# The attribute products of a graph kernel on 64 rows each instead of 128

## What is computed

```python
xn = layernorm(x)
# graph layer: 100,000 edges
m   = concat([xn[src], edge_attr_3], axis=1)          # 256 + 3 columns
tmp = relu(m @ W1.T + b1)
h_N = segment_sum(tmp, dst, num_segments=3125)
gnn = normalise(relu(concat([xn, h_N], axis=1) @ W2.T))
# four layers of linear attention and a 1024-wide feed-forward part on xn
x = x + gnn + mix(xn)
# 16 experts, the two best of each node
x = x + moe(layernorm(x))
```

## Time and profile before

| what | value |
|---|---|
| time, median of 3 runs | 2689.25 us |
| span of the profiled execution, first to last instruction | 2682.9 us |
| PE (matmul) busy | 2088.6 us, 78% of the span |
| PE's weight loads busy | 1673.1 us |
| DVE busy | 1592.4 us, 59% |
| POOL busy | 1338.3 us, 50% |
| ACT busy | 1062.4 us, 40% |
| attribute products (L365) | 142.0 us in 448 matmuls |

### The profile page before, as it was taken

The page is one execution under the profiler, slowest core; times in us unless marked ns, Lnnn a source line. Parts: engine busy times, 40 slices in busy tenths (PEclk is TensorE's granted clock), DMA queues, the critical chain, the costliest instruction groups (busy, mean ns, idle before and its releaser), DMA issues. The chain is left out here.

```text
span 2682.9 us, 44007 instructions
## 1 busy us (share of the span) xinstructions
PE 2088.6 (78%) x10686; PEld 1673.1 (62%) x10686; DVE 1592.4 (59%) x3709; ACT 1062.4 (40%) x2363; POOL 1338.3 (50%) x1224
## 2 busy tenths in 40 slices
PE   1438788997879888978888897888889775599930
PEld 1326667776667666766666776666667565499930
DVE  3747766675776666667666666776667545411126
ACT  1225434443544444444444443544444233133310
POOL 3144556666456555655555566465556600232245
PEclk9769999998999999989899999989999887699975
DMA  6532222223222222232222224222222312499943
GB/s 163 165 90 52 64 61 66 65 66 96 61 65 71 59 61 58 70 97 58 70 63 61 61 68 106 53 62 59 58 59 67 95 53 72 162 335 331 330 149 94
DMA packets 261104, 261.16 MB, mean 97 GB/s; under 512 B 148507, under 2 KB 193426, under 8 KB 260942
## 3 DMA queue, kind: packets, MB, share of 16 engines
q0 software_dynamic: 124672, 132.82, 20.1%
q1 hardware_dynamic: 132158, 126.66, 15.0%
q10 hardware_dynamic: 4112, 0.03, 0.1%
HBM read 229.85 MB, written 28.39 MB: 96 GB/s over the span
## 5 line engine op out<-in xcount | busy, mean ns | idle before, releaser
L426 POOL DMA_INDIRECT G<-P_d,stage x896 | 1147.9, 1281 | 858.8 <-DVE z L405 566.2
L373 ACT ACTIVATE zr<-z 125x512 fp32r<-125x512 f32 x448 | 275.0, 638 | 519.8 <-DVE z L405 350.5
L405 DVE TENSOR_TENSOR z<-bank,G 125x512 f32<-125x512 f32 x448 | 292.7, 686 | 295.9 <-PE bank L365 181.5
L1156 PE MATMUL bank<-TT,W_s 128*128 128x250 f32 (+1 forms) x1280 | 378.1, 447 | 4.7 <-ACT TT L810 3.7
L1027 PE MATMUL bank<-W_s,hid 128*125 128x256 f32 x1600 | 359.6, 379 | 0.0
L1027 PEld LDWEIGHTS bank<-W_s,hid 128*125 128x125 f32 x1600 | 292.6, 187 | 42.8
L1156 PEld LDWEIGHTS bank<-TT,W_s 128*128 128x128 f32 x1280 | 246.1, 199 | 111.6 <-issue 15.9
L379 DVE SCALAR_TENSOR_TENSOR zl<-z,zr 125x512 fp32r<-125x512 f32 x448 | 288.3, 685 | 38.1 <-ACT zr L373 36.8
L357 PE MATMUL bank<-zr,onehot 125*125 125x256 f32 x896 | 268.2, 332 | 10.9 <-DVE zl L379 10.9
L1021 PE MATMUL bank<-ident,hn 125*128 125x125 f32 x700 | 139.5, 309 | 172.2 <-DVE hn L1368 79.7
L810 ACT ACTIVATE TT<-bank,lnc 128x125 f32<-128x125 f32 x600 | 214.5, 476 | 46.2 <-PE bank L1021 46.2
(11 more groups left out here) (284 smaller groups left out, 3125.2 us busy)
## 6 DMA issues: line engine op xcount, KB each, us to landing
W_s<-in_L_ffn_w SPq DMA_DIRECT2D x64, 512.0 KB
hid<-in_L_ffn_w SPq DMA_DIRECT2D x64, 512.0 KB
G<-P_d,stage POOLq DMA_INDIRECT x896
W_s<-in_L_mix_W SPq DMA_DIRECT2D x8, 1024.0 KB
aT<-attr_d SPq DMA_DIRECT2D x224, 31.2 KB
slot_out<-yo SPq DMA_DIRECT2D x32, 128.0 KB
slot_out<-eT SPq DMA_DIRECT2D x32, 128.0 KB
X<-in_x SPq DMA_DIRECT2D x5, 625.0 KB
```

The lines of the kernel that those rows point to most:

```text
L373: nc.scalar.activation(zr[:, s, k, :], z[:, k, :], ACT.Relu).then_inc(r_done, 1)
L405: nc.vector.tensor_tensor(z[:, k, :], edge_bank[k][0:ET, :], G[:, ST * s + 2 * k:ST * s + 2 * k + 2, :].rearrange("p j d -> p (j d)"), ALU ...
L426: nc.gpsimd.indirect_dma_start(G[:, j, :], None, P_d[:, :], bass.IndirectOffsetOnAxis(ap=stage[s][:, j:j + 1], axis=0)).then_inc(g_in[j], 16)
L1156: ins = pe.matmul(to[:, 0:(b - a) * T], W1_s[:, k, part], TT[:, k, TT_PIECES[pc]], start=k == 0, stop=k == KD - 1)
```

## The change

Both operands of each attribute product are cut to the 64 partitions in which that product's weights are not zero: partitions 0 to 63 for `k` = 0, 64 to 127 for `k` = 1. What is cut away is the half of the rows that multiplied zeros. The built program has the same instructions in the same order on every engine; only these 448 matmuls and their weight loads differ. They are marked in it as using a part of the array that is 64 rows by 128 columns, at row 0 and at row 64. All other matmuls of the program but one are marked with the whole array, 128 by 128; the one is that of L498, marked 128 rows by 32 columns.

```diff
@@ -362,7 +362,8 @@
             nc.tensor.wait_ge(at_in[s], group * 16 + 16)
             for k in range(2):
                 nc.tensor.wait_ge(z_done, ge * 2 + (k + 3))
-                nc.tensor.matmul(edge_bank[k][0:ET, :], aT[:, s, :], Wst[:, 2 * k * D:2 * (k + 1) * D],
+                half = slice(64 * k, 64 * k + 64)
+                nc.tensor.matmul(edge_bank[k][0:ET, :], aT[half, s, :], Wst[half, 2 * k * D:2 * (k + 1) * D],
                                  start=True, stop=True).then_inc(e_done, 1)
             if not first:
                 pe_sums(ge - 1, 1 - s)
```

## The result

The changed kernel took 2699.04 us (median of 15 runs, 2691.7 to 2710.62), the kernel before 2690.8 us beside it (15 runs, 2684.78 to 2700.98). The ratio is 1.0034, 95% interval 1.0019 to 1.0049: 9 us slower, with 5 to 13 in the interval. The forecast was 36 us slower. The direction held, but the size was four times too large. That 2699 lies in the stated range says little, since the range of 2671 to 2750 took in "nothing changes" and part of rival 1; the likeliest case's own range, 2709 to 2736, was missed. One of the 12 executions of the kernel with 80 changed pairs (the last experiment) took 5378 us, twice the others, and is in no ratio.

What follows compares the result with a forecast made beforehand. The prediction took PE to bound most of the layers. It added 28 us for `step(1)` to `step(7)`, 6 for the key/value loop and 2 for other pairs: 2689.25 + 36 = 2725 us, range 2671 to 2750.

Steps and rivals of the forecast that it cites:

- nothing changes: Rival for the whole kernel: neither overlap nor a stop, or the two cancel; 2684 to 2694 us, chance 0.13.
- rival 1: Rival: no switching cost and the products overlap, 15 to 31 us faster on 140 pairs; 2658 to 2674, chance 0.23.
- the likeliest case: The forecast itself: each pair 0.14 to 0.25 us dearer, 2725 us in total, own range 2709 to 2736, chance 0.54.
- The mechanism of a pair: At each pair: switching empties the array and uncovers weight loads, while the two products overlap; 0.57 to 0.68 us, not 0.43.
- The pair's price: Each pair of attribute products: 0.14 to 0.25 us more on PE, taken as 0.20.
- The two switches: Into and out of each pair: 0.09 us empty array plus 0.09 us uncovered loading each, 0.36 us together.
- The gain: Within a pair: overlap of the two products saves 0.11 to 0.22 us.
- `step(1)` to `step(7)`, 140 pairs, in PE-bound stretches: Edge steps 1 to 7: the price counts in full, 140 x 0.20 = 28 us.
- The key/value loop: 40 pairs there: only the first product's delay counts, overlap gives nothing back; 20 x 0.18 + 20 x 0.1 = 6 us.
- `step(0)`: 20 pairs in `step(0)`: cost nothing, since PE idles 1.57 us behind them; without that cover 4 us.
- The clock: Granted clock in the layers: stays at 0.94, left out of the sum; a 0.01 shift is worth 18 us.
- The 6.4 us outside the span: Between the span of 2682.9 us and the median of 2689.25: 6.4 us that the change does not touch.

Runs made afterwards that it cites:

- the last experiment: The change applied only to `step(1)` to `step(4)` (80 pairs), or only to the other 144 pairs: ratios 1.0014 and 1.0012 to the kernel before.
- the second experiment: The changed kernel with both attribute products on rows 0 to 63: 2733.44 us, ratio 1.0166 to the kernel before.
- half-gather twins: The kernel before and the changed kernel, each with only every second tile gathered: 2575.13 and 2594.76 us, ratios 0.9563 and 0.9650 to the kernel before.

## Why the prediction was right in direction and four times too large

**The mechanism of a pair** was right in each part. The array is emptied on the way into and out of 64-row products, as it is around the one product at L498: 0.304 instead of 0.210 us ahead of the pair, 0.094, the same as the 0.09 read from the earlier trace rows. The Trainium skill's rule that a change of the tiling mode drains TensorE ("TensorEngine Tiling (Array Packing)", Key Properties) holds for rows too, now with its length. The products overlap, 0.003 to 0.004 us apart, as the Trainium skill says of different row groups ("TensorE: Matmul & The Clock Gate", Part 3); without it the cost would have been 43 us (the second experiment). Rival 1, which rested on that rule alone, fell on the loads: they are not taken under the running matmul of another mode.

**The pair's price** was mis-sized first: 0.125 us, not 0.20. The two switches were put at 0.36 us. They measure 0.094 + 0.05 on the way in, and 0.094 and about 0.10 on the way out (first L358 0.22 us behind its L357, where two such products are 0.12 apart): 0.34. The gain was taken between 0.11 and 0.22 for want of a row; both loads start within 0.003 us of each other, and the gain is the whole 0.21. 140 x 0.125 = 17.5 us instead of 28. The 0.125 lies below even the 0.14 to 0.25 of the prediction, whose 0.20 was a middle value for want of a reading.

**The step that failed** is "`step(1)` to `step(7)`, 140 pairs, in PE-bound stretches": the price was to count in full 140 times. I took an engine that is busy for 17.00 of 17.00 us as the bound of the whole stretch. It was so busy until 985; then came the wait for `hid`, 13.5 us in 14 waits in the 16 passes (4.6 us in 9 in the second profile), which stood in the list of PE's waits and which I left out. What PE lost in `step(1)` to `step(4)`, 4 x 0.125 = 0.5 us a pass, it got back there wherever the pass was held. The half-gather twins show that the gathers set it: with them out of the way all pairs count, and the change costs 20 us. So of the 17.5 us of the 140 pairs some 6 us are found, where the prediction had 28: 5.0 from `step(5)` to `step(7)`, 0.7 in the last passes, 0.5 behind `step(7)`.

The medians of the two profiles of each kernel:

| stretch | before | after | times | us |
|---|---|---|---|---|
| first key/value step to the middle | 87.16, 87.19 | 88.02, 88.01 | 4 | 3.4 |
| `step(1)` to `step(5)`, passes 1 to 4 of a layer | 28.27, 28.08 | 28.19, 28.19 | 16 | about 0 |
| the same, last pass | 20.48, 20.62 | 20.74, 20.73 | 4 | 0.7 |
| `step(5)` to `step(7)` | 13.45, 13.45 | 13.70, 13.70 | 20 | 5.0 |
| `step(7)` to the next `step(0)`, first three | 20.52, 20.64 | 20.83, 20.58 | 12 | not told |
| the same, fourth | 14.89, 14.89 | 15.01, 15.02 | 4 | 0.5 |

9.6 us, against 9 measured. That they agree so well is in part luck. Summed instead of by medians, the second row is 457.5 and 448.3 us before, 451.3 and 451.2 after: 6 us less or 3 us more, by the profile. The fifth row's single values run from 18.6 to 22.6 us, and the stretches from `step(0)` to `step(1)`, which are not listed, differ by 13 us between two profiles of one kernel. The measured 5 to 13 us leave room for this.

**The key/value loop** was put at 6 us and took 3.4. A pass is 0.13 us longer, one pair's price, where 0.28 had been put down. From the first edge step of a pass to the second it is 3.71 us in both kernels, so nothing is added there; the 0.13 comes between the second and the next pass's first (16.39 to 16.51). That the overlap gives nothing back was wrong there: with both products on the same rows this part takes 16.78 us. **`step(0)`** cost nothing, as said, and the wait behind it shrank by the pair's 0.125 us. **The clock** of the layers, whose move from 0.94 was to be a sign of being wrong, reads 0.93 and 0.94 in the two profiles after, and 0.94 and 0.93 in the two before; nothing follows from it, and what the 0.006 over the span costs stays open. **The 6.4 us outside the span** compared two executions: time and span of the same one are some 1.7 to 3.1 us apart. That doesn't touch the difference.

## What to carry to other kernels

In this kernel two products that could share the array were not worth putting side by side between matmuls on the whole array: a switch there and back costs 0.34 us (0.094 of empty array each way, and the weight loads that no matmul covers), and two overlapped products of 512 columns give back 0.21. More such products behind one switch were not tried. Before a term "n times the price" is written down, the whole list of the engine's waits has to be gone through, not its largest entries: a wait of 0.5 to 1 us a pass takes up what four edits of 0.125 us add. And an engine without idle time in a stretch can still be held at the end of it, by a chain through others.

## What the runs showed beyond the question

Half of the gathers less made the kernel 118 us faster, though POOL is busy for only half of the span. More than half of it, some 5.5 us at a time, lies in each of the 12 turns of the loop over `second`: from `step(7)` to the next `step(0)` the median is 20.5 us with all gathers and 15.0 us with half, as in the one passage in each layer where the code goes on without a branch (14.89). In the kernel before, DVE stands there like this, at the turn of the loop:
```profile
1017.89 0.17 DVE L1357 COPY mvA<-mv 125x10 f32 x1 [0.24 <-DVE mv L1342]
1023.08 0.76 DVE L1514 TENSOR_TENSOR X<-bank,X 125x256 f32 x2 [5.01 <-issue]
```
and with half of the gathers like this:
```profile
968.29 0.17 DVE L1359 COPY mvA<-mv 125x10 f32 x1 [0.24 <-DVE mv L1344]
969.01 0.42 DVE L1516 TENSOR_TENSOR X<-bank,X 125x256 f32 x1 [0.54 <-PE bank L1029]
```
5 us without any releaser, gone with the gathers; PE's 12 waits for `X` of the earlier trace rows went with it. Three packets of the instruction queue move in these 12 us of the kernel before and none in the same place of the twin, so that DVE may be waiting for its own code behind the gathers. That was not tried, and stays open. At 12 times 5.5 us it would be worth far more than the change studied here.
